# Two expert stages of a Perceiver block: a copy, a table load and the last sum moved or split at their ends

## The reference: what is computed

```python
def reference(x, ctx_1024, ...):
    x = x + _L0_xattn_ref(_layernorm(x), ctx_1024, ctx_1024)
    x = x + _L0_attn_ref(_layernorm(x), ...)
    x = x + _L0_ffn_ref(_layernorm(x), ...)
    x = x + _L1_xattn_ref(_layernorm(x), ctx_1024, ...)
    x = x + _L1_attn_ref(_layernorm(x), ...)
    x = x + _L1_ffn_ref(_layernorm(x), ...)
    return x

# _L0_ffn_ref: one shared expert and 7 routed ones, the two best per token
    def _swiglu(flat, gate_w, up_w, down_w):
        g = flat @ gate_w.T
        up = flat @ up_w.T
        return jax.nn.silu(g) * up @ down_w.T
    out = _swiglu(flat, shared_gate, shared_up, shared_down)
    for e in range(E_ROUTED):
        eo = _swiglu(flat, routed_gate[e], routed_up[e], routed_down[e])
        routed = routed + combine[:, e:e + 1] * eo
    return (out + routed).reshape(orig_shape)

# _L1_ffn_ref: 16 experts, the three best per token
    hidden = jax.nn.relu(jnp.einsum('btd,edh->bteh', x, W1) + b1)
    expert_out = jnp.einsum('bteh,ehd->bted', hidden, W2) + b2
    return jnp.einsum('bte,bted->btd', gate_topk, expert_out)
```

## Time and profile before

| | |
|---|---|
| median of 3 runs | 513.22 us (513.13 to 517.56) |
| the profiled execution's own time | 514.33 us |
| its span, first to last instruction | 512.5 us |
| mean granted clock of TensorE | 0.967 |
| busy: PE, DVE, ACT, POOL | 88%, 79%, 55%, 23% |

### The profile page before, as it was taken

One profiled execution on the slowest core, in us unless ns is written; L12 is line 12 of the kernel. 1 busy time (PEld: TensorE's weight loads), 2 busy tenths in 40 slices (PEclk: granted clock), 3 DMA queues, 4 the chain that ended last, 5 costly groups with the idle time before them and its releaser, 6 DMA issues.

```text
span 512.5 us, 8716 instructions
## 1 busy us (share of the span) xinstructions
PE 448.9 (88%) x2945; PEld 329.3 (64%) x2945; DVE 404.9 (79%) x1013; ACT 279.5 (55%) x530; POOL 117.8 (23%) x113
## 2 busy tenths in 40 slices
PE   4677598999999999978698879999977999999997
PEld 3343354777778777745345657788766547888885
DVE  4378968776777777676897887889997689999996
ACT  4247025567667766535223398999953336444443
POOL 2003001233123319400000134444420022222220
PEclk9969789999999999999999999999997999999999
DMA  8971000110111010000001000000000107455101
GB/s 279 401 234 40 26 2 1 61 61 1 64 61 61 0 61 1 1 1 1 1 2 41 3 1 2 1 3 2 1 2 1 42 21 271 143 164 157 70 0 42
DMA packets 11096, 29.85 MB, mean 58 GB/s; under 512 B 2529, under 2 KB 4753, under 8 KB 11057
## 3 DMA queue, kind: packets, MB, share of 16 engines
q1 hardware_dynamic: 11056, 29.35, 17.1%
HBM read 28.76 MB, written 0.59 MB: 57 GB/s over the span
## 4 chain that ended last, share of the span: by engine, by line
PE 61%; DVE 20%; ACT 8%; issue 5%; DMA 3%; SPq 2%; DVEq 0%; ACTq 0%
PE pair L403 13%; PE pair L404 13%; PE pair L405 13%; DMA arena<-in_zT 3%; PE pair L794 3%; PE pair L483 2%; PE pair L815 2%; PE pair L820 2%; PE turn L397 1%; PE turn L403 1%; DVE Y L1389 1%; DVE st L1366 1%; ACT arena_r L1136 1%; ACT YT L937 1%; PE turn L405 1%
## 5 line engine op out<-in xcount | busy, mean ns | idle before, releaser
L403 PE MATMUL pair<-yTh,wh 128*128 128x512 f32 x134 | 56.7, 423 | 3.3 <-ACT work L1026 3.2
L1254 POOL TENSOR_TENSOR wl<-wraw,wh 128x512 fp32r<-128x512 f32 x24 | 31.2, 1302 | 113.1 <-ACT wh L959 113.1
L404 PE MATMUL pair<-yTl,wh 128*128 128x512 f32 x134 | 53.0, 395 | 0.0
L405 PE MATMUL pair<-yTh,wl 128*128 128x512 f32 x134 | 52.8, 394 | 0.0
L1623 DVE TENSOR_TENSOR pair<-work,pair 128x512 f32<-128x512 f32 x48 | 33.3, 694 | 24.3 <-PE pair L405 20.4
L483 PE MATMUL pair<-g3b,zerob 128*128 128x512 bf16 x172 | 45.4, 404 | 7.6 <-POOL selb L1232 6.9
L1026 ACT ACTIVATE work<-pair 128x512 f32<-128x512 f32 x64 | 38.3, 599 | 14.5 <-PE pair L405 13.8
L1860 DVE SCALAR_TENSOR_TENSOR pair<-pair,vec,arena 128x512 f32<-128x512 f32 x56 | 42.5, 759 | 2.1
L1050 ACT ACTIVATE ph<-pair 128x512 fp32r<-128x512 f32 x48 | 28.8, 600 | 22.9 <-DVE pair L1623 22.9
L403 PE MATMUL pair<-ph,wh 128*128 128x512 f32 x96 | 38.4, 400 | 2.6 <-DVE pl L1643 2.6
L404 PE MATMUL pair<-pl,wh 128*128 128x512 f32 x96 | 37.7, 393 | 0.0
(11 more groups left out here) (298 smaller groups left out, 1146.5 us busy)
## 6 DMA issues: line engine op xcount, KB each, us to landing
arena<-gates_by_expert SPq DMA_DIRECT2D x14, 512.0 KB, 6.3
wraw<-in_w SPq DMA_DIRECT2D x8, 768.0 KB, 4.3
arena<-in_zT SPq DMA_DIRECT2D x8, 514.0 KB, 9.7
wraw<-in_w SPq DMA_DIRECT2D x7, 512.0 KB, 3.5
arena<-in_z SPq DMA_DIRECT2D x6, 512.0 KB, 12.0
mat<-in_mat SPq DMA_DIRECT2D x1, 776.0 KB, 16.1
hel<-in_mat SPq DMA_DIRECT2D x48, 2.0 KB
row<-in_row SPq DMA_DIRECT2D x1, 576.0 KB, 16.3
```

Of the source, the lines that this page charges most:

```text
L403: pe.matmul(out, ah, bh, start=start, stop=False)
L404: pe.matmul(out, ah, bl, start=False, stop=False)
L405: return pe.matmul(out, al, bh, start=False, stop=stop)
L1254: pool.tensor_tensor(wl[k][:, cols], wraw[:, cols], wh[k][:, cols].bitcast(F32), ALU.subtract)\
```

## The change

In the first expert stage copy_sum of half 0 moves from behind ph(12) to behind ph(13) on ScalarE; its turn_back moves from behind down(13) to behind down(14) on TensorE; the table load moves from behind the waits of step 15 to right behind silu(15). In the second expert stage half 1 of the sum is copied, turned, added and stored in two parts of 256 columns each, the first part's transposes going to bank 1 and the second part's to bank 3.

```diff
--- before.py
+++ after.py
@@ -275,6 +275,8 @@
         GBC0, GATE0, UP0 = bank[0], bank[2], [bank[3], bank[4], bank[5], bank[1]]
         UP1 = bank[2:6]
         BACK = [bank[0], bank[3]]
+        BACK1 = [bank[1], bank[3]]
+        part = lambda ap, p: ap[:, p * HN // 2:(p + 1) * HN // 2]
         LAST0, LAST1 = ((len(s) - n - 1, len(s) - 1) for s, n in ((STEPS0, NF0), (STEPS1, NF1)))
         FREE0 = {"mul": 2, "prod": 4, "down": 2, "xcm": 2, "mm": 2 * NF0, "act": 1}
         FREE1 = {"mul": 2 * NF1, "prod": 4, "down": 4}
@@ -376,10 +378,10 @@
                 for e in range(2 * k + 2, min(2 * k + 4, NE1)):
                     gates(e)
             ov = d["out"].rearrange("(t p) h -> p t h", p=P)
-            for h in range(2):
-                sp.wait_ge(moe[1]["x"], h + 1)
-                sp.dma_start(ov[:, h * HT:(h + 1) * HT, :], X[:, h * HT:(h + 1) * HT, :]).then_inc(stored, 16)
-            sp.wait_ge(stored, 32)
+            for n, ts in enumerate((slice(0, HT), slice(HT, HT + 2), slice(HT + 2, NT))):
+                sp.wait_ge(moe[1]["x"], n + 1)
+                sp.dma_start(ov[:, ts, :], X[:, ts, :]).then_inc(stored, 16)
+            sp.wait_ge(stored, 48)
 
 
         @block.tensor
@@ -544,7 +546,7 @@
                         elif q + 2 >= ready and (not last or q + 2 < len(STEPS0)):
                             up(i, q + 2, last)
                         down(i, q, last and q in LAST0)
-                        if last and q == len(STEPS0) - 3:
+                        if last and q == len(STEPS0) - 2:
                             turn_back(m, 0)
 
                 def first_values():
@@ -636,8 +638,12 @@
                         down(i, q, last and q in LAST1)
 
                 bodies(pe, NE1 // 4, body, 1)
-                for h in range(2):
-                    turn_back(m, h)
+                turn_back(m, 0)
+                for p in range(2):
+                    pe.wait_ge(m["copied"], 2 + p)
+                    for i in (2 * p, 2 * p + 1):
+                        last = pe.transpose(blk(BACK1[p], i), blk(moe_copy(1), i), ident)
+                    last.then_inc(m["back"], 1)
 
             def turn_rows(t):
 
@@ -1031,6 +1037,8 @@
                     k, h, f = STEPS0[q]
                     if not peeled:
                         silu(q)
+                        if last and q == len(STEPS0) - 1:
+                            act.preload_act_table_set(LN_EXP)
                     elif q + 1 < len(STEPS0):
                         silu(q + 1)
                     un = q // NF0
@@ -1045,10 +1053,8 @@
                         weights_hi(m, 2 * i + k + 1, (k + 1) % 2, c, 2 * NF0 * (2 * i + k) + FREE0["down"])
                     act.wait_ge(m["mul"], base + q + 1 + FREE0["mul"])
                     act.wait_ge(m["down"], base + q + FREE0["down"] - 1)
-                    if last and q == len(STEPS0) - 1:
-                        act.preload_act_table_set(LN_EXP)
                     act.activation(ph[q % 2][:, :], UP0[q % 4], ACT.Copy).then_inc(m["hi"], 1)
-                    if last and q == len(STEPS0) - NF0:
+                    if last and q == len(STEPS0) - NF0 + 1:
                         copy_sum(m, 0)
 
             m = moe[0]
@@ -1213,8 +1219,10 @@
             act.wait_ge(m_gtp, 2)
             act.activation(gate_t, bank[5][0:T + NE1, :], ACT.Copy).then_inc(m_gt, 1)
             bodies(act, NE1 // 4, body1, 1)
-            for h in range(2):
-                copy_sum(moe[1], h)
+            copy_sum(moe[1], 0)
+            for p in range(2):
+                act.wait_ge(moe[1]["down"], SUMMED[1][1])
+                act.activation(part(moe_copy(1), p), part(bank[7], p), ACT.Copy).then_inc(moe[1]["copied"], 1)
 
 
         @block.gpsimd
@@ -1872,8 +1880,10 @@
             weigh(0, 0)
             for i in range(NE1 // 4):
                 body1(i, i == NE1 // 4 - 1)
-            for h in range(2):
-                add_experts(m, h)
+            add_experts(m, 0)
+            for p in range(2):
+                dve.wait_ge(m["back"], 2 + p)
+                dve.tensor_tensor(part(half(X, 1), p), part(BACK1[p], p), part(half(X, 1), p), ALU.add).then_inc(m["x"], 1)
 
 
 # ---- launch: lays the inputs out and runs the program on one core ----
```

## The result

The changed kernel takes 0.9945 of the time before, 95% interval 0.9927 to 0.9963, from 22 runs of each: 512.93 us (510.68 to 516.35) against 515.54 us (513.13 to 519.31). By the ratio it is faster by 2.8 us, 1.9 to 3.8. The three runs of before shown ahead of the prediction lay low: with 22 the median is 515.54 and not 513.22.

The account below looks back on a forecast made before the run. The prediction took the kernel as one long dependent program, TensorE holding 61% of the chain, VectorE late from 221.2, the DMA drain setting the end. First stage 1.84 plus tail 0 gave 1.84 us less: 511.4 us, range 510.2 to 513.2.

Parts of the forecast that it names:

- Copy a step later: End of first expert stage: TensorE idles 1.34 us less before gate 14, and multiplication 15 comes 1.38 us earlier.
- The cover of the copy in its new place: First stage, ScalarE: the copy delays SiLU 14, but gate 15 need not wait, with 0.1 to 0.2 us to spare.
- Table load: First stage, ScalarE: load starts behind SiLU 15, multiplication 15 hides 0.7 us; with the copy, remainder 15 comes 2.14 us earlier.
- The rival of the dragging load: First stage: the load waits for the SiLU's pipeline or delays the next activation; 512.4 or 512.5 us, chance 0.08.
- The turn behind product 14: First stage, TensorE: half 0's later transposes make its addition wait, giving back 0.3 of the 2.14 us.
- First stage in all: End of first expert stage: addition of half 0 at 219.97 in place of 221.81, a gain of 1.84 us.
- The wait of the addition for the turn: First stage, VectorE: free at 219.67, the addition of half 0 waits for the transposes until 219.97, about 0.3 us.
- Tail: Kernel end, last sum in two parts: DMA drain stays 1.9 us, so 0 gained; bounds 0.35 less to 0.39 more.
- the gain goes through to the end: From first stage to kernel end: no input DMA lies on the chain, so the 1.84 us go through.
- The rival of the swallowed gain: Behind the first stage: TensorE's fillers or the half 1 chain become late; half the gain, 512.3 us, chance 0.12.
- the end moving by something else than the addition: Sign of a wrong forecast: the kernel's end moves by another amount than the first-stage addition of half 0.
- the rival of falls in other places: TensorE's clock falls in other sparse stretches, each costing at most 1.6 us; two make 514.6 us, slower; chance 0.10.

Follow-up runs that it names:

- e2: Kernel before with only the copy of half 0 a step later in the first stage; ratio 0.9979 (0.9956 to 1.0002) to the kernel before.
- e3: Kernel before with only the table load moved to right behind the last SiLU; ratio 0.9974 (0.9949 to 1.0000) to the kernel before.
- e4: Changed kernel with the first-stage turn of half 0 back behind the product of step 13; ratio 0.9970 (0.9942 to 0.9998) to the kernel before.
- e1: Changed kernel with the three first-stage edits undone, leaving only the last sum in two parts; ratio 0.9999 (0.9969 to 1.0029) to the kernel before.
- e5: Kernel before with a second table load, of another set, ahead of the needed one; ratio 1.0054 (1.0020 to 1.0087) to the kernel before.
- e7: The changed kernel itself, timed once more beside the kernel before on one chip; ratio 0.9943 (0.9911 to 0.9975).
- e6: Changed kernel with half 0 turned behind product 13 in the first stage and ahead of the last product in the second; ratio 0.9956 to the kernel before.

## Why the prediction was right, and where it was off

The time fell, by less than one per cent, and the range held the median, in part by luck: the range stood on 513.22, which lay 2.3 us low, and on the median of the 22 runs the sum would have said 515.54 - 1.84 = 513.70, above the range's 513.2. The median came down into it because the whole gained more than the sum. The steps, one by one:

- Copy a step later: forecast SiLU 13 at 212.19 and gate 14 at 213.37; in the profile after they are at 212.25 and 213.44 in an execution that reaches rounding 12 0.06 later. Alone it gave 1.42 us (e2), forecast 1.38. The cover of the copy in its new place, 0.1 to 0.2 us, held: gate 15 has no idle time before it. Right.
- Table load: forecast to start 0.01 us behind SiLU 15 and to end at 218.42. It starts 0.01 us behind it and ends at 218.46. Alone 0.86 us (e3), forecast 0.87. The rival of the dragging load falls: the load starts within 0.02 us of the activation ahead in the change, in e3 and at 27.83 in the kernel before, and in the first two the next activation starts within 0.02 us of its end. The Trainium skill (ScalarE: Activation LUTs, What ACT_TABLE_LOAD costs) puts a drain of about 1.38 us beside the load; around these loads the traces show none.
- The turn behind product 14: forecast to give back 0.3 us. It does, 0.27 (e4). Right.
- First stage in all: 1.84 forecast, 1.89 in the rows. The wait of the addition for the turn, forecast as 0.3, is 0.18.
- Tail: forecast 0; 0.02 us in the rows, 0.9999 in the ratio (e1). Right, and for the reason given: 512 KB drain in the same 1.9 us. What the prediction left out is that an issue costs up to 0.51 us when stores follow closely, which eats the 0.1 us that SyncE would have had.
- That the gain goes through to the end: right in the mean at one clock (1.9 and 2.1 us; 1.1 of 1.28 for e5). The rival of the swallowed gain, half of it, falls. One of the forecast's own signs of being wrong did show, the end moving by something else than the addition: in the two profiles it moved 512.51 - 511.34 = 1.17 us and the addition 1.83. The two windows around 300 put that down to the clock and not to the stages in between.
- The clock: the rival of falls in other places had the right mechanism with the wrong weight. One longer fall took 0.8 us, where the rival priced one at up to 1.6; over the runs the clock went the other way, the change's mean being higher by what is worth 0.6 to 0.9 us. It did not turn the sign.

What was off is the size of the whole: 1.84 against 2.8 (1.9 to 3.8) by the ratio. The step that failed is the one from the rows of one profiled execution to the median over runs: 513.22 was the median of three runs of which two lay low, and the change's runs had a mean clock higher by 0.002 (against all runs of before in the experiments) to 0.003 (e7), which goes with 0.6 to 0.9 us. At one clock the term is right. Why the change's runs had the higher clock, by chance or through the change, is not shown.

## What to carry to other kernels

Find what stands behind a wait on the same engine, not only what waits: here an off-path copy stood in front of the activation that TensorE's only gate bank was waiting for, and one place further it was free. The table load belonged right behind the last use of the old table, where other engines' work covers a part of it: the move alone gave 0.86 us. Before splitting a last transfer, look whether the DMA engines run dry in front of the last part: at 0.96 busy the split gives nothing, with a hole it gave 0.65 us.

## What the runs showed of the hardware that was not expected

- A run's time follows its mean granted clock closely even in the same kernel: 0.31 us for 0.001, between 0.946 and 0.973. At one clock the standard deviation between runs falls from 1.76 to 0.88 us, so a change of 2 us is better told by rows within one execution than by a dozen runs.
- The second and third of three stores that follow each other closely took 0.51 and 0.49 us to issue in the change, two further apart 0.39 each in the kernel before.
- The stores of 128 KB landed 1.9 us after their issue in e6, where the DMA engines ran dry, and 2.3 us (median of two) in the change, where they stood behind the first store.
